# A six-layer local-attention transformer on one core: the norm's additions on VectorE, and scores in 64x32 tiles

## The reference, cut to what matters

```python
for i in range(DEPTH):   # 6
    x = attn_layer(shift_tokens(x), Wqkv[i], q_scale[i], k_scale[i], Wo[i]) + x
    x = ffn_layer(shift_tokens(x), ln_g[i], ln_b[i], W1[i], b1[i], W2[i], b2[i]) + x

def ffn_layer(x, g, bln, W1, b1, W2, b2):
    mu = x.mean(-1, keepdims=True)
    var = ((x - mu) ** 2).mean(-1, keepdims=True)
    xn = (x - mu) / jnp.sqrt(var + 1e-05) * g + bln
    a, gate = jnp.split(xn @ W1 + b1, 2, -1)
    return a * jax.nn.gelu(gate, approximate=False) @ W2 + b2
```

## Time and profile before

| what | value |
| --- | --- |
| median of three runs | 3271.54 us (3265.06 to 3272.32) |
| span of the profiled execution | 3280.4 us (its own time is not listed apart) |
| instructions | 80720 |
| PE busy | 3087.2 us, 94% |
| DVE busy | 2638.4 us, 80% |
| ACT busy | 2534.1 us, 77% |
| POOL busy | 2084.0 us, 64% |
| 8 steps of the layers (one pass) | 54.01 us |

### The profile page before, as it was taken

How to read it: one execution, slowest core, us unless ns; L and a number is a source line. 1 busy time by engine, 2 the same in 40 slices (tenths; PEclk the granted TensorE clock), 3 DMA queues, 4 the chain that set the end, 5 groups by cost and what they waited for, 6 DMA issues and landing times. The chain is left out here.

```text
span 3280.4 us, 80720 instructions
## 1 busy us (share of the span) xinstructions
PE 3087.2 (94%) x29936; PEld 2736.1 (83%) x29936; DVE 2638.4 (80%) x5117; ACT 2534.1 (77%) x7059; POOL 2084.0 (64%) x1536
## 2 busy tenths in 40 slices
PE   5898886689999999999999999999999999999997
PEld 4666664479998999989999989999899998999996
DVE  3378888878789888788878898878988878888884
ACT  2787885478787888788888888888788887888784
POOL 5347655776666666666666676667676767666661
PEclk8888996799999999999999999999999999999998
DMA  3111100110001000001100011000100000110000
GB/s 128 55 36 49 59 4 7 42 36 11 2 2 34 25 26 2 2 21 33 31 2 2 11 34 39 1 2 2 37 26 22 2 1 21 33 31 7 8 5 26
DMA packets 27780, 75.04 MB, mean 23 GB/s; under 512 B 4120, under 2 KB 9848, under 8 KB 27256
## 3 DMA queue, kind: packets, MB, share of 16 engines
q1 hardware_dynamic: 22224, 52.63, 5.1%
q0 software_dynamic: 4864, 16.78, 1.6%
q10 hardware_dynamic: 304, 0.47, 0.1%
HBM read 65.68 MB, written 4.19 MB: 21 GB/s over the span
## 5 line engine op out<-in xcount | busy, mean ns | idle before, releaser
L1596 POOL TENSOR_TENSOR turned<-by_cos,turned 128x512 f32<-128x512 f32 x384 | 494.5, 1288 | 827.5 <-DVE turned L2101 827.0
L1600 POOL TENSOR_TENSOR rnorm<-norm,half 128x8 f32<-128x8 f32 x384 | 789.1, 2055 | 0.0
L1883 ACT ACTIVATE prob<-ps_s,ebias,rnorm 128x128 f32<-128x128 f32 x1536 | 681.8, 457 | 64.9 <-DVE ebias L2122 64.2
L2115 DVE TENSOR_REDUCE negmax<-ps_s 128x8 f32<-128x1024 f32 x192 | 235.0, 1224 | 284.0 <-PE ps_s L1698 283.9
L1892 ACT ACTIVATE prob_t<-ps_t 128x512 f32<-128x512 f32 x384 | 230.3, 600 | 223.4 <-PE ps_t L1707 218.8
L2130 DVE TENSOR_TENSOR prob<-prob,rinv 128x512 f32<-128x512 f32 x384 | 375.8, 979 | 13.1
L1642 PE MATMUL ps_qk<-w_hi,x_hi 128*128 128x512 f32 x768 | 336.8, 438 | 18.8 <-DVE turned L2101 12.2
L1787 PE MATMUL ps_f<-hid_hi,w_hi 128*128 128x256 f32 (+1 forms) x1056 | 309.3, 293 | 5.7 <-DVE hid_lo L2176 5.6
L1883 ACT ACTIVATION_READ_ACCUMULATOR prob<-ps_s,ebias,rnorm 128x1 f32 x1536 | 311.1, 203 | 0.0
L1642 PE MATMUL ps_qk<-w_lo,x_hi 128*128 128x512 f32 x768 | 305.8, 398 | 0.0
L1642 PE MATMUL ps_qk<-w_hi,x_lo 128*128 128x512 f32 x768 | 305.7, 398 | 0.0
(11 more groups left out here) (289 smaller groups left out, 9779.6 us busy)
## 6 DMA issues: line engine op xcount, KB each, us to landing
w_raw<-in_w_qkv SPq DMA_DIRECT2D x24, 768.0 KB, 4.8
w_raw<-in_w SPq DMA_DIRECT2D x12, 693.0 KB, 4.0
w_raw<-in_w_o SPq DMA_DIRECT2D x12, 512.0 KB, 3.4
w_raw<-in_w SPq DMA_DIRECT2D x6, 768.0 KB, 4.4
x_tok<-in_x SPq DMA_DIRECT2D x8, 256.0 KB, 2.7
kept<-x_t SPq DMA_DIRECT2D x8, 256.0 KB, 2.0
w_raw<-kept SPq DMA_DIRECT2D x8, 256.0 KB, 3.1
out<-rows_out SPq DMA_DIRECT2D x8, 256.0 KB, 2.2
```

Source lines behind the costliest of these rows:

```text
L1596: G.tensor_tensor(turned[:, k, :], by_cos[:, :], turned[:, k, :], ALU.add).then_inc(s["turned"], 1)
L1600: G.tensor_tensor(rnorm[:, i % RR, :], norm2[:, k, :], half[:, :], ALU.pow).then_inc(s["rnorm"], 1)
L1883: last = A.activation(prob[:, k, h, :], half_bank(h % 2, k)[:, T(h // 2)], ACT.Exp, bias=ebias[:, i // NU % 2, k, h:h + 1], scale=rnorm[:, ...
L2115: V.tensor_reduce(negmax[:, k, :, :].rearrange("p u (c o) -> p o u c", o=2), ps_s[:, :, :].rearrange("p o (u c k) -> p o u c k", u=NU, c=2 ...
```

## The change

**The mean and the variance.** After `add_x`, VectorE adds the two halves of `x1` (`halves`, in tile 2 of `hidden`), and `mean_mm` is one matmul on the sum in place of two. After `center`, ScalarE writes the squares to tiles 3 and 4 of `hidden`, and a new VectorE part `add_squares`, directly behind `center`, adds the two (`squares`, tile 2 of `gate`); `var_mm` has two matmuls in place of four. The semaphores `lx1` and `cent` become `x1_and_halves` and `cent_and_squares`, which count both steps.

**Order.** `var_mm` moves to the front of step 2, before `w_2_mm(q, 0)`. The first 9 of the 17 matmuls of `w_2_mm(q, 0)` (tiles 0 to 2) move to the end of step 0, behind `mean_mm`; tiles 3 to 5 (8 matmuls) stay. On ScalarE `square` moves from behind `flip_prob` to before `project` in step 1.

**Scores.** Tiles of 64 rows by 32 columns: four parts of 32 queries in place of two of 64. The mask takes 8 matmuls of 512 columns in place of 4, the products 32 in place of 16. Keys that the mask hides from all 32 queries are left out where that is possible: in the upper half a part has 96 keys in place of 128, and in the first half of the first unit 32 or 64 in place of 64. The order alternates lower and upper parts.

```diff
--- before.py
+++ after.py
@@ -30,6 +30,7 @@
...
 KEPT_RING = 3
+QW = WIN // 2
 GH = 4
...
@@ -1418,7 +1419,7 @@
...
     "qk_square v_copied qk_t prob prob_t attn_hi cent2 lin_hi hid_read_act gelu hid_hi "
-    "qk_by_sin norm2 norm2_floor negmax ebias rinv prob_unit attn_lo lx1 cent spread normed lin lin_lo hid_read_dve gated "
+    "qk_by_sin norm2 norm2_floor negmax ebias rinv prob_unit attn_lo x1_and_halves cent_and_squares spread normed lin lin_lo hid_read_dve gated "
     "fed summed rnorm turned k_unit rstd hid_lo lset"
...
@@ -1472,7 +1473,8 @@
...
     hid_hi, hid_lo = sb("hid_hi", [P, NJ, N]), sb("hid_lo", [P, NJ, N])
-    cent, cent_sq = hidden[:, 0:KT, :], gate[:, 0:KT, :]
+    cent, cent_sq = hidden[:, 0:KT, :], hidden[:, 3:3 + KT, :]
+    halves, squares = hidden[:, KT, :], gate[:, KT, :]
     lin_hi, lin_lo = hid_hi[:, NJ // 2:NJ // 2 + KT, :], hid_lo[:, NJ // 2:NJ // 2 + KT, :]
...
@@ -1673,29 +1675,32 @@
...
                 E.wait_ge(s["dma_c"], 48)
-            for upper in range(2):
+            for part in range(4):
                 for odd in range(2):
-                    rows = slice(WIN * odd, WIN * odd + WIN)
-                    E.matmul(ps_s[upper * WIN:(upper + 1) * WIN, odd, :].rearrange("p (u c k) -> p u c k", u=NU, c=2),
-                             ident_bf[rows, rows], band[rows, upper ^ odd, :, :].unsqueeze(2).broadcast_to([WIN, NU, 2, P]),
-                             start=True, stop=False, skip_group_check=True)
-            for u in range(NU):
-                for c in range(GH // 2):
-                    for upper in range(2):
+                    rows, upper, own = slice(WIN * odd, WIN * odd + WIN), part // 2, part % 2 * QW
+                    E.matmul(ps_s[part * QW:(part + 1) * QW, odd, :].rearrange("p (u c k) -> p u c k", u=NU, c=2),
+                             ident_bf[rows, WIN * odd + own:][:, 0:QW],
+                             band[rows, upper ^ odd, :, :].unsqueeze(2).broadcast_to([WIN, NU, 2, P]),
+                             start=True, stop=False, skip_group_check=True, tile_position=(WIN * odd, QW * part))
+            for c in range(GH // 2):
+                for u, upper in ((1, 0), (0, 1), (1, 1), (0, 0)):
+                    for part in (2 * upper, 2 * upper + 1):
                         for odd in range(2):
                             rows = slice(DH * odd, DH * odd + DH)
-                            first = u * P + upper * WIN
-                            q_win = qk_t[rows, c, first:first + WIN]
+                            q_part = qk_t[rows, c, u * P + part * QW:][:, 0:QW]
                             k_all = qk_t[rows, 2 + c, :]
-                            o = half_bank(odd, u)[upper * WIN:(upper + 1) * WIN, T(c)]
+                            o = half_bank(odd, u)[part * QW:(part + 1) * QW, T(c)]
                             if upper:
-                                k_win = k_all[:, T(u)]
+                                seen = slice((part - 2) * QW, (part + 1) * QW)
+                                k_seen, o = k_all[:, T(u)][:, seen], o[:, seen]
                             elif u:
-                                k_win = k_all[:, WIN:WIN + P].rearrange("p (w k) -> p w k", w=2)[:, ::-1, :]
+                                k_seen = k_all[:, WIN:WIN + P].rearrange("p (w k) -> p w k", w=2)[:, ::-1, :]
                                 o = o.rearrange("p (w k) -> p w k", w=2)
                             else:
-                                k_win, o = k_all[:, 0:WIN], o[:, 0:WIN]
-                            last = E.matmul(o, q_win, k_win, start=False, stop=True, skip_group_check=True)
+                                seen = slice(0, (part + 1) * QW)
+                                k_seen, o = k_all[:, seen], o[:, seen]
+                            last = E.matmul(o, q_part, k_seen, start=False, stop=True, skip_group_check=True,
+                                            tile_position=(DH * odd, QW * part))
             last.then_inc(s["scores"], 1)
...
@@ -1743,21 +1748,17 @@
...
         def mean_mm(q):
-            E.wait_ge(s["lx1"], q + 1)
+            E.wait_ge(s["x1_and_halves"], 2 * q + 2)
             if q:
...
                 E.wait_ge(late["ostate"], B)
-            for kt in range(KT):
-                last = E.matmul(ps_f[1][:, 0:N], mean_w[:, :], shifted(x1[:, q % 2, :])[:, kt, :], start=kt == 0, stop=kt == KT - 1)
-            last.then_inc(s["mean"], 1)
+            E.matmul(ps_f[1][:, 0:N], mean_w[:, :], halves, start=True, stop=True).then_inc(s["mean"], 1)
 
         def var_mm(q):
-            E.wait_ge(s["cent2"], q + 1)
+            E.wait_ge(s["cent_and_squares"], 2 * q + 2)
             for u in range(NU):
-                for kt in range(KT):
-                    last = E.matmul(ps_f[1][:, N + u:N + u + 1], cent_sq[:, kt, T(u)], mean_w[:, 0:1], start=kt == 0,
-                                    stop=kt == KT - 1)
+                last = E.matmul(ps_f[1][:, N + u:N + u + 1], squares[:, T(u)], mean_w[:, 0:1], start=True, stop=True)
             last.then_inc(s["var"], 1)
...
@@ -1788,35 +1789,36 @@
...
 
-        def w_2_mm(q, mt):
+        def w_2_mm(q, mt, tiles):
             if q % B == 0:
                 E.wait_ge(s["low"], OTHER * (q // B + 1))
-            E.wait_ge(s["lx1"], min(q + 2, PASSES))
-            for j in range(NJ):
+            E.wait_ge(s["x1_and_halves"], 2 * min(q + 2, PASSES) - 1)
+            for j in tiles:
                 if j % 3 == 0:
...
                                     x[:, j, :].bitcast(F32R), start=j + n == 0, stop=j == NJ - 1 and n == 1)
-            last.then_inc(s["out_ps"], 1)
+            if NJ - 1 in tiles:
+                last.then_inc(s["out_ps"], 1)
 
...
                 hidden_mm(q, 0)
+            for q in passes(t, 18):
+                var_mm(q)
             for q in passes(t, 26):
-                w_2_mm(q, 0)
+                w_2_mm(q, 0, range(3, NJ))
             for q in passes(t, 20):
...
             for q in passes(t, 27):
-                w_2_mm(q, 1)
+                w_2_mm(q, 1, range(NJ))
             for i in units(t, 2):
...
                 rstd_row_mm(q)
-            for q in passes(t, 18):
-                var_mm(q)
             for c in lates(t, 14):
...
@@ -1831,6 +1833,8 @@
...
                 mean_mm(q)
+            for q in passes(t, 24):
+                w_2_mm(q, 0, range(3))
             for q in passes(t, 14):
...
@@ -1901,9 +1905,9 @@
...
         def square(q):
-            A.wait_ge(s["cent"], q + 1)
+            A.wait_ge(s["cent_and_squares"], 2 * q + 1)
             if q:
-                A.wait_ge(s["hid_lo"], 2 * q)
+                A.wait_ge(s["gated"], 2 * q)
             A.activation(cent_sq, cent[:, :, :], ACT.Square).then_inc(s["cent2"], 1)
...
@@ -1993,6 +1997,8 @@
...
                 head_mirror(c, 1)
+            for q in passes(t, 17):
+                square(q)
             for i in units(t, 0):
...
@@ -2005,8 +2011,6 @@
...
                 heads_out(c)
-            for q in passes(t, 17):
-                square(q)
             for c in lates(t, 13):
...
@@ -2142,7 +2146,12 @@
...
             V.tensor_tensor(whole(x1[:, q % 2, :]), ps_f[0][:, :].rearrange("p (k n) -> p k n", k=KT), whole(state[:, q % B, :]),
-                            ALU.add).then_inc(s["lx1"], 1)
+                            ALU.add).then_inc(s["x1_and_halves"], 1)
+            V.wait_ge(s["x1_and_halves"], 2 * q + 1)
+            if q:
+                V.wait_ge(s["gated"], 2 * q - 1)
+            by_half = shifted(x1[:, q % 2, :])
+            V.tensor_tensor(halves, by_half[:, 0, :], by_half[:, 1, :], ALU.add).then_inc(s["x1_and_halves"], 1)
 
...
@@ -2150,7 +2159,13 @@
...
             V.tensor_tensor(cent[:, :, :], shifted(x1[:, q % 2, :]), ps_f[1][:, 0:N].unsqueeze(1).broadcast_to([P, KT, N]),
-                            ALU.subtract).then_inc(s["cent"], 1)
+                            ALU.subtract).then_inc(s["cent_and_squares"], 1)
+
+        def add_squares(q):
+            V.wait_ge(s["cent2"], q + 1)
+            if q:
+                V.wait_ge(s["hid_lo"], 2 * q - 1)
+            V.tensor_tensor(squares, cent_sq[:, 0, :], cent_sq[:, 1, :], ALU.add).then_inc(s["cent_and_squares"], 1)
 
...
@@ -2311,6 +2326,8 @@
...
                 center(q)
+            for q in passes(t, 17):
+                add_squares(q)
             for q in passes(t, 22):
```

## The result

The changed kernel takes **3303.18 us** (median of 4 runs, 3300.42 to 3305.18) against 3271.09 (3265.06 to 3272.32, 4 runs): ratio **1.0095**, 95% interval 1.0077 to 1.0112. It is slower by 0.95%, by its medians 32 us; 3268 was predicted. The profiled execution took 3305.18, its span 3303.8 (3280.4 before). The first `project` of the layers starts at 585.68 and the last at 3211.52 (592.96 and 3191.75 before), so the layers are longer by 27 us; the front was shorter by 7 in this execution, the tail longer by 4.

The account below looks back on a forecast made before the run. PE, 99% busy, was taken to set the pace, if its inputs come early enough. Steps 0 to 2 losing 24 us and scores gaining 27 gave -3, so 3268 us; range 3224 to 3312, likeliest case 3252 to 3280.

Parts of the forecast that it names:

- the scores' gain: PE's score block in steps 3, 5 and 7: 64x32 tiles save 0.19 us per group, 27.4 us in all.
- if eight tiles run side by side: Condition of the 0.19 us per score group: row halves and column quarters, each seen alone, also work combined.
- Its path: In steps 3, 5 and 7 what follows hangs on the scores' end, so a shorter block shortens the pass.
- records can't be issued that fast: Rival, chance 0.14: issue pace limits the 64 score records per group; slower, 3317 us at 15.7 ns or 3418 at 26.6.
- the tiles don't gain and don't lose: Rival, chance 0.08: eight score tiles share something four already fill; only the 24 us loss stays, 3295 us.
- The blocked addition: VectorE's squares' addition before `negmax` waits for all of GpSimd's `hid_lo`; `project` 0.24 us later, steps 0 to 2 lose 24 us.
- Step 1: PE's step 1 starts 0.32 us later, as 9 moved matmuls follow the shortened mean; its score gain lies before the wait.
- The first rival: The squares' addition on VectorE isn't blocked: 0.52 us gained in each of 30 passes, 3228 us; chance 0.20.
- Steps 1 and 2 of the heavy passes: In the 18 of 48 passes that also split weights, `project` comes about 0.95 us later through the blocked addition, 17.1 us.
- covered: VectorE's addition of the halves costs 0.41 us before `prob`, but PE's `flip_prob` at 2931.83 hides the delay.
- bound of 30 us: Upper bound of the loss in steps 0 to 2, if VectorE is also late at step 3's scores where weights split.
- a gap of 1 us: PE stands idle for about 1 us before each `project` of step 2, released by the sines.

Follow-up runs that it names:

- e4: The changed kernel with every score matmul cut to 32 key columns, so it computes something else; 3268.62 us, a single run.
- e8: The changed kernel with the squares added by a one-input reduction and `center` moved ahead of `gate_value(q, 1)` on VectorE; 3272.55 us, ratio 0.9982 to the kernel before.
- e3: The changed kernel with the squares added by a one-input `tensor_reduce` in place of a two-input `tensor_tensor`; 3276.07 us, ratio 0.9996 to the kernel before.
- after: The changed kernel itself, with all parts of the change; 3303.18 us, ratio 1.0095 to the kernel before.
- e2: The changed kernel with the old scores in 64x64 tiles; 3307.93 us, ratio 1.0095 to the kernel before.
- e12: e10, but with the 9 `w_2_mm` matmuls moved only in five of eight passes; 3261.32 us, ratio 0.9946 to the kernel before.
- e9: The kernel before with only the mean from added halves and the 9 moved `w_2_mm` matmuls, old variance and scores; 3272.95 us, ratio 0.9987.
- e10: e9 with the 64x32 scores, tiles visited in the order of e7; 3270.35 us, ratio 0.9977 to the kernel before.
- e1: The kernel before with only the new 64x32 scores; 3272.03 us, ratio 0.9993 to the kernel before.
- e7: e1 with the score tiles' column parts visited in turn; 3271.85 us, ratio 0.9996 to the kernel before.
- e11: e1 with the tiles reordered so that narrow score matmuls come first in each half; 3275.45 us, ratio 0.9988 to the kernel before.

## Why the prediction was wrong

**The failed step is the scores' gain**, 27.4 us. Its condition "if eight tiles run side by side" holds at the start: in the trace the eight masks start within 0.024 us. Its path holds too, by e4. But the step priced a block of 64 records by its columns alone. Measured is 0.02 per group (1.21 to 1.19), not 0.19: all 64 starts took 0.783 us, nearly as long as the 32 of the kernel before, 0.775. Why they keep this pace the runs don't settle. The rival "records can't be issued that fast" had put the point from which nothing is gained at 13.3 ns per record, which 12.4 nearly reaches, but its prices at 15.7 and more. The case that came is "the tiles don't gain and don't lose", 3295 us, to which I had given 0.08. The Trainium skill (TensorE: Matmul & The Clock Gate, Part 1) states about 25 ns between starts as a floor. The runs show 3 to 4 ns between the masks, which go to different tiles, and 9.4 on average over 40 records of e4, so for different tiles the floor does not hold here.

**The blocked addition came as computed.** It ends 0.28 after `hid_lo` and takes 1.96 us (0.28 and near 1.9 were forecast), and `project` of a light pass is later by 0.28 (0.24 forecast). Step 1 was forecast later by 0.32, a sum whose terms give 0.35; it is 0.19 later from the mean to `flip_qk` (1.50 us for 1.31). That did no harm, since the chain hangs on `hid_lo`. The Trainium skill (SBUF — State Buffer, "Who interferes with whom") says that the second of such a pair is fully blocked, whichever it is. The runs agree both ways, by the addition here (1.96 us) and by `hid_lo` in e8 (3.31). The same section of the Trainium skill says that a reduction never contends, and e3 agrees (0.71 us). The first rival fell, but its price was nearly right: freed by e3, the light periods gain 0.47 (10.9 / 23) where 0.52 had been put.

**Steps 1 and 2 of the heavy passes** lose 1.35, 0.80 and 0.94 us in the third layer's first three passes, 1.03 on average where 0.95 was forecast; the fourth loses 0.28 as a light one does. The size came out, but in part by luck, since not all of it is the wait that was priced. Of the 1.35, step 1 has 0.91, which the forecast had put down as covered. From step 0's `project` to `flip_prob` it is 0.51 longer (2.91 us for 2.40): the halves are not covered there, because at a layer's start VectorE has also the new layer's tables (L2033, L2036) ahead of `prob`. The other 0.40 lie between `flip_prob` and the next `project`, where the moved matmuls stand. VectorE, then PE, of the changed kernel:
```profile
1459.54 0.43 DVE L2154 TENSOR_TENSOR hidden<-x 128x256 f32<-128x256 f32 x1
1459.88 0.42 DVE L2033 TENSOR_TENSOR cos_t<-rot_cos,qk_gain 128x256 f32<-128x256 f32 x1
1460.22 0.48 DVE L2036 TENSOR_TENSOR sin_t<-rot_sin,qk_gain 128x128 f32<-128x128 f32 x2
...
1460.95 0.69 DVE L2134 TENSOR_TENSOR prob<-prob,rinv 128x512 f32<-128x512 f32 x1
```
```profile
1461.70 0.66 PE L1712 MATMUL ps_t<-ident,prob 128*128 128x128 f32 x4 [0.57 <-DVE prob L2134]
```
And under the blocked addition lay a second wait, for `center` and the square, which the forecast did not name: in e3 `negmax` still starts 1.30 us after `center`'s end.

**Past step 2** nothing but the scores was forecast to change; only the bound of 30 us allowed for a late VectorE in step 3. In fact step 3 at a layer's start takes 5.99 us instead of 5.36, at the lower clock, and step 4 of a layer's third pass 8.73 instead of 8.27, of which I did not look for the cause. The nine matmuls had been PE's work in the wait for `hid_lo`; the forecast took their 1.06 us as saved, named only a gap of 1 us ahead of `project`, and had no fall of the clock in it.

In sum the norm and the moved matmuls cost 27 to 29 us (the layers' span, first to last `project`, in after and in e2: 27.1 and 29.3 longer) where 24 were forecast, and the scores gave next to nothing where 27 were forecast: 3 us faster became 32 slower. The last 3 to 5 of the 32 are not placed; the tail was 3.6 longer in the profiled execution, and front and tail differ by as much between kernels that are the same there.

## What to carry to other kernels

Count records as well as columns before packing a matmul block finer: here 64 records in eight tiles took as long as 32 in four, with a quarter fewer columns on the fullest tile. Before adding a VectorE instruction with two SBUF inputs look for the GpSimd instruction that runs there, and once it is moved, for the next pair that then meets (here the weights' low parts and `hid_lo`). Work that PE does inside a long wait is worth keeping there even where lighter passes gain by moving it: the order may differ by pass.

## What the runs showed of the hardware that I had not expected

- `w_lo`, 1.76 us alone, took 3.25 beside a `hid_lo` that had started 0.71 before it; that `hid_lo` itself took 2.34 instead of 1.82, having started 0.68 before the end of the copy `w_hi`, which took 1.37 instead of 0.95.
- The clock at the first heavy pass of a layer, by PE's idle time before it: 1.30 us, no fall in 5 layers (kernel before); 1.34, none in 5 (e12); 1.74, a fall to 0.50 in 4 of 5 (e3); 2.06, in 2 of 5 (e9); 2.08, in 3 of 5 (e10); 2.28, in all 5 (after). In e8, with 1.25 us, a block and another 0.55, it fell in all 5. So the longest idle time alone doesn't order the cases. In the changed kernel it fell 0.5 to 1.2 us after PE had started again.
- In e1's block the first eight score records, all for different tiles, start within 0.023 us. Over the whole block it is 12.4 ns from start to start, and 12.4 and 12.5 with the tiles in two other orders (e7, e11). With 32 columns each it is 8.8 ns (e4).
